# Moving the multiplication by 1/std from the turned tokens to the projected keys and queries

## The reference

```python
def reference(x, w_attn, w_proj, decay_raw, W1, W2, Wr):   # x: 8 x 512 x 128
    xn = _layernorm(x)                                     # (x - mean) / std
    return x + attn(xn, w_attn, w_proj, decay_raw) + ffn(xn, W1, W2, Wr)

def attn(x, w_attn, w_proj, decay_raw):
    q, k, v = jnp.split(x @ w_attn, 3, axis=-1)            # then heads: 16 of 8 columns
    ...
    logw = -jnp.log1p(softplus(decay_raw)[:, None, None] * log1p_dist)
    scores = einsum('bhqd,bhkd->bhqk', q, k) / sqrt(8) + causal + logw
    y = einsum('bhqk,bhkd->bhqd', softmax(scores), v)
    return y.reshape(B, T, C) @ w_proj

def ffn(x, W1, W2, Wr):                                    # 8 experts, the best 2 of each token
    ...
```

## Time and profile before

| | us |
|---|---|
| median of 3 runs | 511.52 |
| lowest, highest | 511.45, 512.29 |
| profiled execution | 511.92 |
| its span | 510.0 |
| mean granted TensorE clock | 0.981 |

### The profile page before, as it was taken

The page is one execution under the profiler, slowest core; times in us unless marked ns, Lnnn a source line. Parts: engine busy times, 40 slices in busy tenths (PEclk is TensorE's granted clock), DMA queues, the critical chain, the costliest instruction groups (busy, mean ns, idle before and its releaser), DMA issues.

```text
span 510.0 us, 13402 instructions
## 1 busy us (share of the span) xinstructions
PE 479.3 (94%) x4284; PEld 346.6 (68%) x4284; DVE 365.6 (72%) x1401; ACT 336.5 (66%) x620; POOL 364.0 (71%) x592
## 2 busy tenths in 40 slices
PE   6859899999999999989999999999999999999993
PEld 5735565555665565556566656599999999998552
DVE  6797989988999989979889888823333333334695
ACT  5948878888887888877988888843233323233860
POOL 2398887889888888879889889635455454555782
PEclk9967999999999999999999999999999999999997
DMA  6596690780471461443253253877676766661823
GB/s 186 148 340 200 181 224 11 215 197 19 139 204 33 137 205 31 142 137 98 98 166 119 76 168 97 236 240 227 208 210 201 211 203 198 195 209 39 325 68 103
DMA packets 72738, 82.22 MB, mean 161 GB/s; under 512 B 8622, under 2 KB 52688, under 8 KB 72672
## 3 DMA queue, kind: packets, MB, share of 16 engines
q1 hardware_dynamic: 68352, 72.91, 49.2%
q0 software_dynamic: 4320, 8.47, 4.7%
HBM read 49.94 MB, written 31.86 MB: 160 GB/s over the span
## 4 chain that ended last, share of the span: by engine, by line
PE 62%; DVE 18%; ACT 7%; POOL 5%; issue 3%; SPq 2%; DMA 2%; ACTq 0%; DVEq 0%; POOLq 0%
PE psT L1450 17%; PE psT L1528 13%; PE ps L1501 12%; DVE scores L1248 9%; PE psO L1472 8%; PE ps L1422 5%; ACT probs L989 3%; POOL scores L859 3%; DVE x_all L599 2%; POOL rows_dram L871 2%; ACT scores L944 2%; PE psM L1398 2%; PE ps L1492 1%; SPq L736 1%; DVE xt L1105 1%
## 5 line engine op out<-in xcount | busy, mean ns | idle before, releaser
L1248 DVE CUSTOM_DVE_ANT_0 scores<-ps,wdist 128x256 f32<-128x256 f32 (+3 forms) x512 | 217.2, 485 | 24.0 <-PE ps L1422 23.4
L989 ACT ACTIVATE probs<-psT 128x512 f32<-128x512 f32 x320 | 173.8, 596 | 51.9 <-PE psT L1450 50.8
L859 POOL TENSOR_SCALAR scores<-scores,row_max 128x256 f32<-128x256 f32 (+3 forms) x388 | 183.2, 487 | 33.7 <-DVE row_max L1248 32.6
L1450 PE MATMUL psT<-ident,scores 128*128 128x128 f32 x1280 | 177.8, 282 | 6.1 <-ACT probs L989 5.0
L1450 PEld LDWEIGHTS psT<-ident,scores 128*128 128x128 f32 x1280 | 138.8, 142 | 64.2 <-issue 44.3
L878 POOL DMA_INDIRECT picked_dram<-scores,row_ring x71 | 69.8, 983 | 70.6 <-DVE scores L1301 67.3
L998 ACT ACTIVATE scores<-ps 128x512 f32<-128x512 f32 x71 | 42.4, 597 | 91.9 <-PE ps L1501 91.9
L1472 PE MATMUL psO<-probs,values 128*32 128x512 f32 (+3 forms) x1024 | 88.4, 441 | 0.0
L944 ACT ACTIVATE scores<-scores,row_max 128x512 f32<-128x512 f32 x124 | 82.9, 726 | 0.0
L1501 PE MATMUL ps<-scores,wdist 128*128 128x128 f32 x568 | 75.2, 275 | 1.4 <-DVE scores L1289 1.1
L1528 PE MATMUL psT<-xn_all,scores 128*128 x568 | 75.7, 276 | 0.6 <-ACT scores L998 0.5
(11 more groups left out here) (152 smaller groups left out, 292.2 us busy)
## 6 DMA issues: line engine op xcount, KB each, us to landing
wdist<-w1t SPq DMA_DIRECT2D x71, 256.0 KB, 3.3
k_rows<-k_dram SPq DMA_DIRECT2D x64, 96.0 KB, 2.8
q_rows<-q_dram SPq DMA_DIRECT2D x64, 96.0 KB, 2.6
row_ring<-rows_dram SPq DMA_DIRECT2D x71, 65.0 KB, 3.3
rows_dram<-row_ring SPq DMA_DIRECT2D x6, 650.0 KB, 6.4
k_dram<-k_parts SPq DMA_DIRECT2D x7, 384.0 KB, 2.4
q_dram<-q_parts SPq DMA_DIRECT2D x7, 384.0 KB, 2.6
wdist<-picked_dram SPq DMA_DIRECT2D x4, 512.0 KB, 6.6
```

The costliest lines, as they stand in the source:

```text
L859: last = nc.gpsimd.tensor_scalar(part, part, -1.0, row_max[:, r, tile, quad:quad + 1], ALU.mult, ALU.add)
L989: nc.scalar.activation(probs[:, at.ring(2), w, :], psT[:, w % 2], ACT.Exp, scale=-1.0).then_inc(exp_ready, 1)
L1248: last = nc.vector.tensor_tensor_reduce(out=scores[:, r, u, col:col + n], in0=bank[:, col:col + n], in1=wdist[:, at.g * QUADS + quad, SEQ ...
L1450: last = nc.tensor.transpose(psT[:, w % 2, place * P:(place + 1) * P], scores[:, at.ring(2), u, col + key * P:col + (key + 1) * P], ident[:])
```

## The change

XN is gone. K's matmul takes the turned tokens as they come, and a new step KX (QX for Q) on DVE multiplies the result in its bank: `psM *= yt`. This is the same product, since 1/std belongs to the token, which is a column of the bank. Batch 0 isn't concerned (its tokens are normalised beforehand).

ScalarE's first copy is taken out of KA and becomes a step KH of its own, which waits for KX (`parts_scaled`). The steps behind it each stand one place later in the slot: KH where KR was, KR behind p1(2), KM behind the third pair TE(4, 6), KL behind p1(4). YT, which overwrites `yt`, now waits for QX; K's matmul waits for the load of `xt` rather than for XN.

```diff
@@ slot_steps
     per_batch("KA", -3)
     per_batch("QA", -2)
     per_batch("VR", -2)
     per_batch("V", -1)
+    if n != 1:
+        per_batch("KX", -3)
+    per_batch("QX", -2)
     per_batch("YT", 6)
...
     step("PV", n - 2, NGROUP, 1)
-    per_batch("KR", -3)
-    per_batch("QR", -2)
+    per_batch("KH", -3)
+    per_batch("QH", -2)
     step("TE", n - 1, NGROUP, 2, 4)
...
-    per_batch("KM", -3)
-    per_batch("QM", -2)
     per_batch("PJ", 7)
...
     p1(2)
+    per_batch("KR", -3)
+    per_batch("QR", -2)
     p1(3)
     step("TE", n - 1, NGROUP, 4, 6)
+    per_batch("KM", -3)
+    per_batch("QM", -2)
+    step("PV", n - 2, NGROUP, 2)
+    p1(4)
     per_batch("KL", -3)
     per_batch("QL", -2)
-    step("PV", n - 2, NGROUP, 2)
-    p1(4)
-    per_batch("XN", -4)
...
@@ ScalarE, hi_step
                         act.wait_ge(misc_full, at.misc(kind, 1))
+                        if at.c > 0:
+                            act.wait_ge(parts_scaled, at.batches(2, number - 2))
...
@@ VectorE
-                def scale_tokens(at):
...
-                    v.tensor_tensor(xt[:, at.parity, :], xt[:, at.parity, :], yt[:], ALU.mult).then_inc(xt_scaled, 1)
+                def scale_step(kind):
+                    def step(at):
+
+                        dve.wait_ge(scales_loaded, at.batches(16))
+                        dve.wait_ge(misc_full, at.misc(kind, 1))
+                        v.tensor_tensor(psM[:], psM[:], yt[:], ALU.mult).then_inc(parts_scaled, 1)
+                    return step
...
@@ VectorE, turn_back
                     dve.wait_ge(y_scaled, at.batches(GROUPS // PAIR, GROUPS // PAIR))
+                    if at.c + 2 * GROUPS < NGROUP:
+                        dve.wait_ge(parts_scaled, at.batches(2, 4))
...
@@ TensorE, all_heads_step
                         if kind == "KA" and at.c > 0:
-                            pe.wait_ge(xt_scaled, at.batches(1))
+                            pe.wait_ge(xt_copied, 2)
+                            if at.c > GROUPS:
+                                pe.wait_ge(xt_loaded, at.batches(16, -16))
```

More of the change, by code:

```diff
@@ L88 @@
              2: (("CZ", 1),) + tuple(("LC", b * GROUPS) for b in range(6)),
-             3: (("XN", 4),),
              4: (("V0", 0), ("RS", 3), ("LC", 24), ("LC", 28), ("CZ", 2)) + tuple(
@@ L165, in per_batch @@
             b = (n - phase) // GROUPS
-            if 0 <= b < BATCH and b >= {"XT": 2, "V": 1, "RB": 2, "XN": 2}.get(kind, 0 if kind in ("YT", "PJ") else 1):
+            if 0 <= b < BATCH and b >= {"XT": 2, "V": 1, "RB": 2}.get(kind, 0 if kind in ("YT", "PJ") else 1):
                 steps.append((kind, b * GROUPS - n))
@@ L489, in build @@
         scales_loaded = sem("scales_loaded")
-        xt_scaled = sem("xt_scaled")
+        parts_scaled = sem("parts_scaled")
         misc_full = sem("misc_full")
@@ L662, in scales_load @@
                     if b == 2:
-                        sp.wait_ge(xt_scaled, 1)
+                        sp.wait_ge(parts_scaled, 2)
                     if b >= 3:
@@ L945, in less_act_step, with hi_step @@
                                              bias=row_max[:, r, TILES - 1, quad:quad + 1]).then_inc(less_act, 1)
-                def hi_step(kind, parts, written, first_written):
+                def hi_step(kind, number, parts, written, first_written):
                     def step(at):
                         act.wait_ge(misc_full, at.misc(kind, 1))
+                        if at.c > 0:
+                            act.wait_ge(parts_scaled, at.batches(2, number - 2))
                         if at.c > 0:
@@ L998, in hidden_step @@
                     nc.scalar.activation(hidden_t[:, s % 2], ps1[:, s % 2], ACT.Silu).then_inc(hidden_ready, 1)
-                parts = {"KA": hi_step("KA", k_parts, k_written, k_first), "KM": mid_step("KA", 1, k_parts),
-                         "QA": hi_step("QA", q_parts, q_written, q_first), "QM": mid_step("QA", 2, q_parts),
+                parts = {"KH": hi_step("KA", 1, k_parts, k_written, k_first), "KM": mid_step("KA", 1, k_parts),
+                         "QH": hi_step("QA", 2, q_parts, q_written, q_first), "QM": mid_step("QA", 2, q_parts),
                          "V": v_step, "TE": exp_step, "WC": centred_copy, "RT": rstd_copy,
@@ L1094, in first_values @@
                                   v_stage(0)[:, :, 0:C].rearrange("p t (h d) -> p t h d", d=HD)).then_inc(first_v_ready, 1)
-                def scale_tokens(at):
[L1098 to L1104, removed]
-                    v.tensor_tensor(xt[:, at.parity, :], xt[:, at.parity, :], yt[:], ALU.mult).then_inc(xt_scaled, 1)
+                def scale_step(kind):
[4 more added lines that the diff above has]
+                    return step
                 number_parts = {"VL": wide_copy,
                                 "KR": rest_step("KA", 1, k_parts), "KL": lo_step("KA", 1, k_parts),
-                                "QR": rest_step("QA", 2, q_parts), "QL": lo_step("QA", 2, q_parts), "XN": scale_tokens, "V0": first_values}
+                                "QR": rest_step("QA", 2, q_parts), "QL": lo_step("QA", 2, q_parts), "KX": scale_step("KA"), "QX": scale_step("QA"), "V0": first_values}
                 run_prologue({**number_parts, "BN": norm_stats, "WC": scaled_weights, "NX": normalise})
```

## The result

The changed kernel is slower by more than forecast: 521.14 us (median of 4 runs, 520.57 to 521.43) against 511.90 us (4 runs, 511.45 to 513.10) for the kernel before. The ratio is 1.0173, 95% interval 1.0154 to 1.0192. The forecast was 514.7 us, with a range of 511.8 to 517.0. The profiled execution took 521.35 us, its span 519.3.

A forecast was written before the change was run, and what follows sets the result against it. From slot 9 on TensorE's own work was taken to bound the kernel, so DVE changes count only through TensorE's waits. The terms, -2.3 + 3.3 + 0.85 + 0.9 + 0 + 0 = +2.75 us, added to 511.92 gave 514.7 us, range 511.8 to 517.0.

The forecast's parts named there:

- Term 1: Slots 13 and 17: TensorE's waits behind the long XN multiplies go away, -2.3 us.
- Term 2: Slots 10, 14 and 22: QH waits for QX with exponentials queued behind it, so TensorE stops, +1.1 us each.
- rival of the shorter stop: Slots 10, 14, 22: only DVE's own 0.64 us delay on p1(2) remains, ahead of p1(4); 512.5 us, chance 0.17.
- Term 3: Slot 26, on the way to the experts through GpSimd: GpSimd ends late, +0.85 us.
- Term 4: Slot 6: a TensorE stop of 1.5 us that swallows 0.58 of later waits for DVE, +0.9 us.
- Term 5: Slot 18: the 1.1 us stop lies under the existing wait for the first sends to land, 0 (0 to 0.3) us.
- term 6: Slots 0 to 3: earlier first exponentials against a stop in slot 2, 0 us (-1.4 to +0.7).
- slower still: K slots' 0.1 us margins give way, 515.9 us, or new multiplies stretch beside GpSimd, 519 us; chance 0.12.

The follow-up runs named there:

- sr_late: Changed kernel with SR, DVE's step that waits for the first sends to land, moved behind QL in slot 18; 516.99 us, ratio 1.0056 to 1.0104.
- kl_early: Changed kernel with KL alone moved back ahead of p1(4), QL staying behind it; 516.32 us, ratio to the kernel before 1.0042 to 1.0091.
- before_kl_late: Kernel before with KL alone moved behind p1(4), no multiply added or removed; 514.08 us (one execution).
- Combined: Changed kernel with QH behind TE(2, 4), SR behind QL and YT one slot later; 513.68 us, ratio to the kernel before 1.0017 to 1.0052.
- steps_only: Changed kernel's step order with XN kept and no multiply in the bank; 518.15 us, ratio to the kernel before 1.0084 to 1.0154.
- after_again: Changed kernel profiled a second time with no edit; 520.97 us (one execution).
- yt_later: Changed kernel with YT alone moved one slot later, from phase 6 to phase 7; 520.66 us (one execution).

## Why the prediction was wrong

**Term 1 held** (-2.3 forecast, -2.32 measured): slots 13 and 17 became like slot 21. The new multiplies are fourteen rows of one form, none stretched:

```profile
L1107 DVE TENSOR_TENSOR psM<-psM,yt x14: 694/695/699, 39.2 to 303.2; 128x512 f32<-128x512 f32 x14
```

XN had reached 2.93 us. By the Trainium skill (SBUF — State Buffer, "SBUF: two separate sides") an instruction with one input in PSUM is not held up by a GpSimd instruction that reads SBUF; the 14 rows agree, seven of them beside element-wise instructions of GpSimd in whole or part, the others beside its sends. XN met GpSimd in every slot. In slots 12 and 16 it was XN that waited, through five subtractions; in slots 4, 8, 20 and 24 it took 0.69 to 0.81 us, and GpSimd's 128x128 subtraction beside it 0.80 to 0.87 instead of 0.36.

**Term 2 held** (+1.1 each forecast, +1.12 measured), by its mechanism, its place and its gap (1.06 us). The experiments show that the stop follows the multiply's own time (0.53 us less for 0.53 us less of multiply) and its place, and show behind it the 0.6 us of the rival of the shorter stop. K's slots cost nothing on TensorE from slot 9 on, as said; slot 5, for which I had 0 as well, grew by 0.44.

**Term 3** was sized by GpSimd's slack at 0.85; all of slot 26's 1.11 arrived (GpSimd's last send of rows stands 25.02 us behind the start of slot 26 instead of 23.96). **Term 4** was +0.9 and came out at +0.57: slot 5 grew by 0.44, slot 6 by 0.62 and slot 7 gave back 0.49. How it is divided varies (sr_late, the same kernel up to there, has slot 5 at 10.31 and slot 6 at 12.35 us), the sum doesn't (+0.57).

**Term 5 is the step that failed**: "This cause keeps its place in time, the 1.1 us stop comes ahead of it in the same slot and lies under it", with 0 to 0.3 us; measured +3.45 and +4.48. The send did keep its place in time (4.2 us into the slot), but not its length, and the stop of 1.06 us did not lie under its wait but was added to it; even in kl_early, where the send lands in 2.29 us, slot 18 is 0.59 us longer than before. The fault was made earlier, in K's slots: "KL moves behind p1(4) in the same stretch and costs nothing more". I costed KL by DVE alone. It releases K's write and with it the loads behind it in SyncE's queue; for Q I looked at this and asked only when the loads are needed, not what else is in flight then. The rows for it were there: DVE and TensorE both waited in slot 18 for a landing, and the loads' last issue was 1.8 us ahead of the send, a lead that the moved steps took away. Which of the transfers delays the send was not separated; that they do when they come with it is shown from both sides (kl_early, before_kl_late). The second half of the error is the clock: I took a longer wait at its own length, and behind it TensorE's work took 1.6 us more.

**The rest of the miss** is not settled. Of the 6.7 us between 514.7 and the profiled 521.35, slot 18 is 3.45, the start 1.40 and the experts' stage 1.65. The start of slot 0 came 1.40 us later because TensorE's clock rises later in the prologue: in both profiles its matmuls start at the same times up to 6 us and take 0.42 us each, and they fall to 0.28 us at 6.1 us before and at 9.2 after. The first row is of before, the second of after, 6 to 9 us from the start; their clock column says 1.00 in both, since the profile's account of the clock only begins with the rise:

```profile
6.00:9.00 3.00, 3.00 (x23) 2.54 (x21) 1.56 (x12) 2.25 (x6) 1.05 (x1) 1.00 1.08 302
```

```profile
6.00:9.00 3.00, 3.00 (x12) 2.37 (x11) 0.59 (x6) 0.74 (x3) 1.05 (x1) 1.00 1.10 305
```

TensorE gets 23 matmuls done in one and 12 in the other. Over all kernels slot 0 starts anywhere between 24.76 and 26.16 us, in the order in which the clock rises (6.1 to 9.2 us): 24.76 to 25.79 in the four profiles with the old prologue and steps, 24.90 to 26.16 in the ten with the moved ones. Combined, whose prologue is the changed kernel's, had its rise at 6.4 us. So this varies from one execution to the next, and whether the change shifts it too is open. The same holds for the experts' stage: 146.9 to 147.9 us in the former, 147.2 to 150.0 in the latter. Slots 0 to 3, term 6, added 0.53 and 1.06 us in the two profiles, inside its bounds in one (-1.4 to +0.7) and outside in the other; slot 4 added nothing in one and 0.51 in the other. The clock differs here too: its mean over slots 0 to 4 is 0.87 before, 0.94 and 0.91 after, so that the changed kernel was longer there in spite of a faster clock. Slot 2 alone added 1.33 and 1.52; I had let a wait of 0.79 us, in slot 3, take up the stop there, and slot 3 gave back 0.39.

The chances were wrong in the same way: "slower still" had 0.12 and two mechanisms, neither of them a DMA, although the change moves two steps, KL and QL, that release transfers.

## What to carry to other kernels

A moved step is costed with everything it releases: the DMAs it sets free, what is queued behind them, and whatever other transfer is in flight at the new time, above all one whose landing an engine already waits for. A copy that waits for a new producer goes behind the work that doesn't need it, on an engine that works in order; one line for QH was worth 0.5 us in each of four slots. And a change that is slower as it stands may be held back by a few places only: with QH, SR, YT and PJ moved, the kernel with the same multiply is 0.6% faster than before instead of 1.7% slower. About half of the 0.6% is SR's move, which gives the kernel before 0.3% without any multiply moved.

## What the runs showed of the hardware

The send took 2.27 us (kernel before) and 2.29 us (kl_early) to land where the DMA engines were 0.44 and 0.34 busy in the 2 us from its issue, and 4.24 and 4.18 us (changed kernel, before_kl_late) where they were 0.92 and 0.91 busy, with loads in flight. The Trainium skill (DMA: Bandwidth & Descriptors, "Queues, rings and completion order") says that each DMA engine takes turns between the queues that it has work for, a packet at a time; a send from GpSimd's queue would then take turns with SyncE's loads. The landings agree with it, though no run here shows the turns themselves.

A wait can cost more than its length. Behind single TensorE gaps of 2.50 (before_kl_late) and 3.16 us (steps_only) in slot 18, and behind 1.06 and 1.99 in the changed kernel, the granted clock was 0.50 for some 3.4 us and slot 18's mean 0.88; around 1.06 and 2.13 us in after_again it was 0.50 for 6.8 us and the mean 0.79; behind 1.20 us in the kernel before, and behind 1.06 and 1.59 in yt_later, it stayed at 1.00. Of the 3.45 us that slot 18 lost in the changed kernel, 1.60 were this.
